# Attention's output projection as three fp32r products of upper parts and remainders

## The reference, cut to what matters

```python
x = x + _L1_xattn_ref(_layernorm(x, axis=-1), ctx_1024, ctx_1024, mask, L1_xattn_W_out)
...
energy = jnp.einsum('nqhd,nkhd->nhqk', q, k)
...
attn = jax.nn.softmax(energy / jnp.sqrt(jnp.float32(EMB)), axis=-1)
out = jnp.einsum('nhqk,nkhd->nqhd', attn, v).reshape(N, Q, EMB)
return out @ W_out.T
```

## Time and profile before

| | |
|---|---|
| Median of 3 runs | 818.58 us (815.93 to 818.9) |
| The profiled execution | 820.4 us, of which span 818.6 us |
| TensorE busy | 693.6 us, 85% of the span |
| VectorE busy | 633.1 us, 77% |
| ScalarE busy | 486.2 us, 59% |
| GpSimd busy | 313.5 us, 38% |
| Projection's products (L1540) | 128 records in eight steps |

### The profile page before, as it was taken

The page is one execution under the profiler, slowest core; times in us unless marked ns, Lnnn a source line. Parts: engine busy times, 40 slices in busy tenths (PEclk is TensorE's granted clock), DMA queues, the critical chain, the costliest instruction groups (busy, mean ns, idle before and its releaser), DMA issues.

```text
span 818.6 us, 11765 instructions
## 1 busy us (share of the span) xinstructions
PE 693.6 (85%) x4143; PEld 533.0 (65%) x4143; DVE 633.1 (77%) x1244; ACT 486.2 (59%) x621; POOL 313.5 (38%) x249
## 2 busy tenths in 40 slices
PE   6881039999999878999999999999999999019998
PEld 5760026898888744566556656577887887018998
DVE  5998885887877388887677685988887999996554
ACT  2222013444453436796896887656655997996773
POOL 4354503476677644233421420003531443792000
PEclk9996559999999989999999999999999999558999
DMA  8927714456634570010023000004210834101433
GB/s 296 332 94 249 241 36 131 111 139 179 167 67 57 110 240 1 1 47 27 1 70 106 7 21 26 26 27 155 103 51 27 281 106 152 52 0 52 141 117 103
DMA packets 59540, 84.95 MB, mean 104 GB/s; under 512 B 7904, under 2 KB 47712, under 8 KB 57952
## 3 DMA queue, kind: packets, MB, share of 16 engines
q1 hardware_dynamic: 49936, 61.09, 22.4%
q0 software_dynamic: 7872, 21.11, 10.6%
q10 hardware_dynamic: 1680, 2.08, 0.7%
HBM read 53.73 MB, written 30.54 MB: 103 GB/s over the span
## 4 chain that ended last, share of the span: by engine, by line
PE 62%; DVE 14%; ACT 7%; issue 4%; POOL 3%; DMA 1%; POOLq 0%; DVEq 0%; ACTq 0%
PE bank L2096 13%; PE bank L2358 9%; PE bank L2152 9%; PE bank L2382 5%; PE bank L1446 4%; PE bank L1480 3%; PE bank L1503 3%; PE bank L1540 3%; PE bank L1500 3%; DVE above L781 2%; PE bank L1461 2%; PE bank L1484 2%; ACT wgateT L2045 1%; DVE qx L1177 1%; ACT qT L1329 1%
## 5 line engine op out<-in xcount | busy, mean ns | idle before, releaser
L1303 ACT ACTIVATE x<-bank,bic 128x512 f32<-128x512 f32 x160 | 106.2, 697 | 34.8 <-PE bank L1480 32.5
L1177 DVE TENSOR_REDUCE qx<-bank 128x4 fp32r<-128x616 f32 x128 | 98.1, 797 | 28.2 <-PE bank L1446 26.8
L2096 PE MATMUL bank<-ux,uwh 128*128 128x512 f32 x384 | 96.5, 392 | 0.2 <-ACT ux L1990 0.2
L2096 PEld LDWEIGHTS bank<-ux,uwh 128*128 128x128 f32 x384 | 72.5, 189 | 16.0 <-issue 0.6
L1480 PE MATMUL bank<-qT,K 128*128 128x512 f32 x128 | 62.1, 495 | 3.4 <-ACT x L1303 2.0
L1446 PE MATMUL bank<-Kb,qTb 128*128 128x308 bf16 x256 | 54.6, 306 | 5.8 <-DVE qx L1177 3.4
L2319 ACT ACTIVATE wgateT<-bank 128x512 f32<-128x512 f32 x32 | 19.2, 599 | 65.9 <-PE bank L2358 61.9
L1104 POOL CAST qx<-q 128x1024 fp32r<-128x1024 f32 x8 | 8.5, 1068 | 116.5 <-PE bank L1461 107.7
L2096 PE MATMUL bank<-ux,uwl 128*128 128x512 f32 x192 | 52.2, 394 | 0.0
L2358 PE MATMUL bank<-xh,wh 128*128 128x512 f32 x128 | 49.9, 390 | 0.3 <-issue 0.3
L2358 PE MATMUL bank<-xl,wh 128*128 128x512 f32 x128 | 50.0, 390 | 0.0
(11 more groups left out here) (420 smaller groups left out, 2026.9 us busy)
## 6 DMA issues: line engine op xcount, KB each, us to landing
xs_dram<-ux POOLq DMA_DIRECT2D x6, 1024.0 KB, 4.2
ux<-xs_dram POOLq DMA_DIRECT2D x6, 1024.0 KB, 5.2
x_dram<-x SPq DMA_DIRECT2D x4, 1024.0 KB, 5.6
xr<-in_w1T SPq DMA_DIRECT2D x8, 512.0 KB
xr<-in_w3T SPq DMA_DIRECT2D x8, 512.0 KB
xr<-in_w2T SPq DMA_DIRECT2D x8, 512.0 KB
row_dram<-xn SPq DMA_DIRECT2D x8, 512.0 KB, 3.2
x_dram<-xr SPq DMA_DIRECT2D x8, 512.0 KB, 2.9
```

Of the source, the lines that this page charges most:

```text
L1177: dve.tensor_reduce(qx[:, k, g * GH:(g + 1) * GH, MROW].rearrange("p (u h) -> p u h", u=2), pair[i][:].rearrange("p (u x) -> p u x", u=2)[ ...
L1303: act.activation(pr[g % 2][h], S_[u % 2], ACT.Exp, bias=bic[:, s // 2, h // GH:h // GH + 1]).then_inc(p_done, 1)
L2096: mm = pe.matmul(bank[j][:, m * TB:(m + 1) * TB], w[:, c * HI + cols:c * HI + cols + P], x[:, part, c * TB:(c + 1) * TB], start=(w is uwh ...
```

## The change

The attention result and the weights are each split: the upper part is the value rounded to fp32r (`attH`, `woH`), the remainder is the value less that (`attL`, `woL`). Three fp32r products per block and half of the features replace one fp32 product: upper by upper, upper by weight's remainder, remainder by weight's upper part.

ScalarE's copy writes `attH` (and counts in a semaphore of its own, `at_hi`); a new job y of VectorE, `feature_remainders`, subtracts it from what is in the pair and adds to `done`. In the drain both are in halves, and ScalarE's second copy waits for the first subtraction. The weights are copied by ScalarE and subtracted by VectorE once, at the start. The tables change too: in steps 1 to 7 TensorE's maximum 11 is ahead of the projection, which is a slot later, at slot 10, with two turns of queries behind it, and maximum 12 behind these; y is in VectorE's lists behind maximum 10, in step 7 behind the second attention normalization and in the drain behind the norms H. The order of uses of the pairs becomes: a, m, m, w, q, q, m. Buffers move: `q` and the raw weights take places that are free then.

```diff
--- before.py
+++ after.py
@@ -986,8 +986,9 @@
             pr = [[place(5 * i + h, 1) for h in range(GH + 1)] for i in range(2)]
             ob = [place(10 + i, 1) for i in range(2)]
             att = place(12, 2).rearrange("p (k d) -> p k d", k=QT)
-            attT = place(14, 2).rearrange("p (c t) -> p c t", c=DC)
-            woT, V0 = sb(st, "woT", [P, DC, D]), sb(st, "V0", [P, HEADS, 2 * HD])
+            q = place(14, 2).rearrange("p (k h d) -> p k h d", k=QT, h=HEADS)
+            wo_raw = place(12, 1).rearrange("p (c e) -> p c e", c=DC)
+            woH, V0 = sb(st, "woH", [P, DC, D], F32R), sb(st, "V0", [P, HEADS, 2 * HD])
             sb(st, "rows_place", [P, 32])
             qx = sb(st, "qx", [P, QT, HEADS, SW], F32R)
             K = [K0, sb(st, "K1", [P, PR, 2, P], F32R)]
@@ -999,8 +1000,10 @@
             Kb = [Kb0, sb(st, "Kb1", [P, G, GH, S2], BF16)]
             V = [V0, sb(st, "V1", [P, HEADS, 2 * HD])]
             Vr = [sb(st, f"Vr{i}", [P, G, P]) for i in range(2)]
-            q = sb(st, "q", [P, QT, HEADS, HD])
             raw = sb(st, "kraw", [P, PR, S2]), sb(st, "kbraw", [P, G, S2])
+            attH = sb(st, "attH", [P, DC, QN], F32R)
+            attL, woL = sb(st, "attL", [P, DC, QN], F32R), sb(st, "woL", [P, DC, D], F32R)
+            at_hi = sem("at_hi")
             v_in = [sem(f"v_in{i}") for i in range(2)]
             f_in, x3_out = [sem(f"f_in{s}") for s in range(NQ // 2)], sem("x3_out")
             EARLIER = 16 * (NS // RING)
@@ -1019,15 +1022,15 @@
                         "x": ("xt", 0), "W": ("split", 0), "S": ("table", 0), "R": ("root", 0)}
             DVE_WORK = {"m": ("mx", 1), "n": ("norm", 0), "A": ("wo", -1), "v": ("var", -1), "x": ("mask", 0), "r": ("rest", 0),
                         "M": ("mx", 0), "Y": ("query", 0), "s": ("stat", 0), "R": ("root", 0),
-                        "H": ("final", 0), "L": ("last", -1), "E": ("end", 0), "N": ("normal", 0), "P": ("peak", 0)}
+                        "y": ("low", -1), "H": ("final", 0), "L": ("last", -1), "E": ("end", 0), "N": ("normal", 0), "P": ("peak", 0)}
             FIRST_PE = ("M", "MMM", "MQMMM", "MM", "M", "QM", "BQ", "", "mm", "mm", "", "", "", "mm", "mm", "mm", "m", "m", "mqm", "mqmqbq")
-            LATER_PE = ("mm", "m", "m", "m", "mm", "mm", "m", "am", "", "wWm", "qm", "q", "", "qm", "", "m", "m", "", "b", "q")
+            LATER_PE = ("mm", "m", "m", "m", "mm", "mm", "m", "am", "", "m", "wWq", "qm", "", "qm", "", "m", "m", "", "b", "q")
             FIRST_ACT = ("", "", "Q", "", "", "B", "Q", "ooCQ", "", "", "", "", "", "", "o", "", "", "ob", "q", "qqcq")
             LATER_ACT = ("", "", "o", "", "", "", "", "o", "fk", "", "k", "q", "oq", "", "q", "", "b", "o", "", "cq")
-            FIRST_DVE, SECOND_DVE, LATER_DVE = "sRYMMMMssRMMMnMMMMMMMMMxsmmmmnsmmmmmmmmmnmmnm", "ssmmmmmmmnmmmsmRAmnmrmmmnnv", "mmmmmmmnmmmnmAmmxrmnmmnv"
+            FIRST_DVE, SECOND_DVE, LATER_DVE = "sRYMMMMssRMMMnMMMMMMMMMxsmmmmnsmmmmmmmmmnmmnm", "ssmmmmmmmnmmmsmyRmAnmrmmmnnv", "mmmmmmmnmmmmynmAmxrmnmmnv"
             END_PE = ("", "", "x", "", "x", "a", "x", "wW", "x", "x", "x", "x", "x")
             END_ACT = ("", "", "o", "x", "xS", "", "", "f", "xW", "x", "x", "Rx", "x", "x")
-            LAST_DVE, END_DVE = "HNPnNPNPnANPvnNPn", "NPnHNPLENP"
+            LAST_DVE, END_DVE = "HNPnNPNPnyNPnAvNPn", "NPnHyNPLENP"
 
             def by_step(s, first, later, end):
                 table = first if s == 0 else end if s == NQ else later
@@ -1065,7 +1068,7 @@
             def attention_sync(sp):
                 sp.wait_ge(e_yw, YW)
                 value_loads(sp, 0)
-                sp.dma_start(woT[:], a["woT"].rearrange("(c p) e -> p c e", p=P)).then_inc(w_in, 16)
+                sp.dma_start(wo_raw, a["woT"].rearrange("(c p) e -> p c e", p=P)).then_inc(w_in, 16)
                 sp.wait_ge(e_put, PUT)
                 for t in range(0, QT, 2):
                     sp.dma_start(xr[:, t, :], tiles(x2_dram)[:, t, :]).then_inc(rows_in[t], 16)
@@ -1247,7 +1250,20 @@
                     dve.tensor_reduce(peak[:, s:s + 1], xr[:, s * QT:(s + 1) * QT, :], AX.XY, ALU.max,
                                       apply_absolute_value=True).then_inc(h_am, 1)
 
+                def feature_remainders(s):
+                    if s < 0:
+                        return
+                    i, n = TURN["at", s, 0]
+                    for half in range(1 if s < NQ - 1 else 2):
+                        cols = slice(half * 2 * P, (half + 1) * 2 * P) if s == NQ - 1 else slice(0, QN)
+                        dve.wait_ge(at_hi, s + half + 1)
+                        dve.tensor_tensor(attL[:, :, cols], pair[i][:].rearrange("p (c t) -> p c t", c=DC)[:, :, cols],
+                                          attH[:, :, cols].bitcast(F32), ALU.subtract).then_inc(
+                            at_half if s == NQ - 1 and half == 0 else done[i], 1)
+
                 dve.memset(qb[:, :, :, HD:HD + 1], 1.0).then_inc(f_one, 1)
+                dve.wait_ge(w_in, 17)
+                dve.tensor_tensor(woL[:], wo_raw, woH[:].bitcast(F32), ALU.subtract).then_inc(w_in, 1)
                 def work(kind, s):
                     i = count[kind, s] = count.get((kind, s), -1) + 1
                     if kind in ("stat", "root", "final", "normal", "peak"):
@@ -1264,6 +1280,8 @@
                         normalized(G * s - 1 + i)
                     if kind == "query":
                         first_queries()
+                    if kind == "low":
+                        feature_remainders(s)
                     if kind == "wo" and 0 <= s:
                         added(s)
                     if kind == "var" and 0 <= s:
@@ -1342,12 +1360,13 @@
                         if s:
                             wait_full(act, "wo", s - 1, 0)
                         if s < NQ - 1:
-                            act.copy(attT.rearrange("p c t -> p (c t)"), pair[i][:]).then_inc(done[i], 1)
+                            act.copy(attH[:], pair[i][:].rearrange("p (c t) -> p c t", c=DC)).then_inc(at_hi, 1)
                         else:
                             for half in range(2):
                                 cols = slice(half * 2 * P, (half + 1) * 2 * P)
-                                act.copy(attT[:, :, cols], pair[i][:].rearrange("p (c t) -> p c t", c=DC)[:, :, cols]).then_inc(
-                                    done[i] if half else at_half, 1)
+                                if half:
+                                    act.wait_ge(at_half, 1)
+                                act.copy(attH[:, :, cols], pair[i][:].rearrange("p (c t) -> p c t", c=DC)[:, :, cols]).then_inc(at_hi, 1)
 
                 def normal_turned(b):
                     i, n = TURN["xt", b, 0]
@@ -1365,6 +1384,8 @@
                 act.wait_ge(e_put, PUT)
                 for t in range(1, QT, 2):
                     act.dma_start(xr[:, t, :], tiles(x2_dram)[:, t, :]).then_inc(rows_in[t], 16)
+                act.wait_ge(w_in, 16)
+                act.copy(woH[:], wo_raw).then_inc(w_in, 1)
 
                 def filler(kind, s):
                     i = count[kind, s] = count.get((kind, s), -1) + 1
@@ -1530,15 +1551,16 @@
                             wait_done(pe, "at", s, 0)
                         else:
                             pe.wait_ge(at_half, 1)
-                        pe.wait_ge(w_in, 16)
+                        pe.wait_ge(w_in, 18)
                     else:
                         i, _ = TURN["wo", s, 0]
                         dst, sent = pair[i], full[i]
                         wait_done(pe, "at", s, 0)
                     for k in (2 * half, 2 * half + 1):
                         for c in range(DC):
-                            mm = pe.matmul(dst[:, k * D:(k + 1) * D], attT[:, c, k * P:(k + 1) * P], woT[:, c, :],
-                                           start=(c == 0), stop=(c == DC - 1))
+                            for x, w in ((attH, woH), (attH, woL), (attL, woH)):
+                                mm = pe.matmul(dst[:, k * D:(k + 1) * D], x[:, c, k * P:(k + 1) * P], w[:, c, :],
+                                               start=(c == 0 and x is attH and w is woH), stop=(c == DC - 1 and x is attL))
                     if half:
                         mm.then_inc(sent, 1)
                     elif s == NQ - 1:
```

## The result

| | before | after |
|---|---|---|
| Median of 4 runs each, same chip | 818.03 us (815.93 to 818.9) | 830.32 us (829.28 to 831.73) |
| Ratio | | 1.0157, 95% interval 1.0135 to 1.0179 |
| The profiled execution, and its span | 820.4, 818.6 us | 830.78, 829.0 us |
| First product of the feed-forward starts | 554.4 us | 569.0 us |
| The last stage lasts | 69.4 us | 66.2 us |

What follows compares the result with a forecast made beforehand. TensorE was taken to bound the attention's steady part. Steps 1 to 6 (+4.75 us) and step 7 with the drain (+5.65) summed to +10.4 on the median 818.58, so 829.0 us, range 821 to 834.

Runs made afterwards that it cites:

- experiment 1: Changed kernel, but in steps 0 to 6 ScalarE's copy releases the pair and the subtraction reads only SBUF (features' remainder zero): 828.15 us, 1.0157.
- experiment 3: Changed kernel with step 7's subtraction earlier in VectorE's list, behind the second normalization and peak; addition and statistics move with it: 827.18 us, 1.0136.
- experiment 4: Kernel before, fp32 products and no subtraction, with the changed kernel's order of TensorE's and VectorE's lists: 828.5 us, 1.0141.
- experiments 6: Changed kernel with key copies later, maximum 11 behind slot 10's values, and step 1's maximum 11 and addition ahead of the norms: 827.22 us, 1.0121.
- 8: Changed kernel with only ScalarE's key copies moved later: 830.31 us, 1.0159.
- 11: Changed kernel's computation with TensorE's order of before; subtraction behind maximum 10, in step 7 behind the second normalization and peak: 828.55 us, 1.0128.
- 7: Changed kernel with later key copies and maximum 11, step 1 list reordered, earlier subtraction in step 7 and drain: 822.12 us, 1.0074.
- experiment 9: Changed kernel's computation reordered: key copies in slots 3 and 5, projection in slot 12, VectorE's lists to match: 822.81 us, 1.0058.

## What to carry to other kernels

Before an instruction of the bounding engine is moved past other work, list what the other engines do while it runs at its old place: each of those jobs loses its cover, and this can cost more than the wait that the move was meant to hide. A wait taken away is worth only the distance to the one that ends next, as the odd steps in experiment 1 showed. And where TensorE stands for microseconds ahead of a job, price that job at both clock levels.

## What the runs showed of the hardware

- The granted clock fell within the attention's last steps: after 2.54 us of standing still step 7's projection ran at 0.52, 24 products in 5.04 us for 2.82. Filled with other products, the same wait left it at 1.00.
- The length of the idle time ahead does not settle it: in the drain TensorE stood 3.10 us in the changed kernel and ran at 1.00, and 3.09 us in experiment 3 and ran at 0.66 (2.81 and 4.25 us). The wait of 2.54 us ahead of step 7's products gave 5.04 us after and 4.23 in experiment 1; one of 1.60 us gave 5.03 in steps 1 and 3 of experiment 4 and full clock in step 5. Most repairs of the lists had the low clock at another projection or at one more: 5.07 us in the drain of experiments 6 and 8, 5.08 in 11, 4.34 in 7 and 9. What decides stays open.
- The last stage, with the same 576 products, took 65.4 to 69.4 us over fourteen kernels, more than most of the effects here. It has two parts. The low clock at its start, where there was any, cost up to 1.7 us. And at a granted clock of 1.00 a product of 128x256 started every 0.118 us in five kernels and every 0.113 in nine, which is 2.4 us over the stage. What chooses stays open, and whether it goes with the kernel or with the single execution wasn't tried.
- fp32r products of 128x256 cost 0.122 us each in the projection at full clock (2.81 us for 23 distances), 0.118 in experiment 9, against 0.43 for the fp32 product; a subtraction 128x1024 out of PSUM with fp32r result 1.21 to 1.23 us, as the addition of that size.
